# Gate products on an added weight, a matmul tile issued earlier, and the order of four engines around a recurrent attention block

## The reference, cut to what matters

```python
x = x + _L1_ffn_ref(_layernorm(x), ...)            # stage D: 256 -> 704 -> 256, gelu gate
x = x + _L2_xattn_ref(_layernorm(x), ctx, ctx, Wi, bi, Wf, bf, ln_scale)   # stage E
x = x + _L2_ffn_ref(_layernorm(x), weight, bias)   # stage F: ternary weights, 8-bit activations
x = x + _L3_xattn_ref(_layernorm(x), ctx, ...)     # stage G
```

```python
x = jnp.concatenate([q, k, v], axis=-1)            # k = v = ctx
ig = (x @ Wi + bi); fg = (x @ Wf + bf)             # 16 heads each
log_f = log_sigmoid(fg); log_f_cum = cumsum(log_f)
D = exp(log_D - max(log_D));  C = (q k^T) / 4 * D  # 64 heads (4 batches x 16)
h = (C / normaliser) @ v;  normalise per head
```

## Time and profile before

| | us |
|---|---|
| median of 3 runs (lowest, highest) | 1100.76 (1100.33, 1102.03) |
| the profiled execution, its own time | 1100.16 |
| its span in the profile | 1098.2 |
| PE, DVE, ACT, POOL busy | 1031.1, 873.1, 621.4, 567.2 |
| granted TensorE clock, mean | 0.984 |

### The profile page before, as it was taken

How to read it: one execution, slowest core, us unless ns; L and a number is a source line. 1 busy time by engine, 2 the same in 40 slices (tenths; PEclk the granted TensorE clock), 3 DMA queues, 4 the chain that set the end, 5 groups by cost and what they waited for, 6 DMA issues and landing times.

```text
span 1098.2 us, 19095 instructions
## 1 busy us (share of the span) xinstructions
PE 1031.1 (94%) x6570; PEld 877.5 (80%) x6570; DVE 873.1 (80%) x2154; ACT 621.4 (57%) x1657; POOL 567.2 (52%) x412
## 2 busy tenths in 40 slices
PE   8999999999998999889878999999999999999988
PEld 6458888888886786566556888998889988999976
DVE  6367777777778856599998888888887898888885
ACT  1774444444332356678656667665776666766643
POOL 4246666677652232044345665646565565655640
PEclk9999999999999999889989999999999999999999
DMA  7011101111000012000000101010100101000201
GB/s 268 1 46 66 58 29 58 37 52 58 30 1 27 1 56 77 2 1 1 20 1 19 59 1 40 1 59 1 34 7 2 58 2 39 2 20 1 88 1 39
DMA packets 15008, 37.43 MB, mean 34 GB/s; under 512 B 1649, under 2 KB 6849, under 8 KB 14401
## 3 DMA queue, kind: packets, MB, share of 16 engines
q1 hardware_dynamic: 14912, 36.21, 9.9%
HBM read 35.16 MB, written 1.05 MB: 33 GB/s over the span
## 4 chain that ended last, share of the span: by engine, by line
PE 66%; DVE 22%; ACT 6%; issue 4%; POOL 2%; DMA 0%; DVEq 0%; SPq 0%; ACTq 0%; POOLq 0%
PE bank L743 15%; PE bank L765 8%; PE bank L2160 8%; PE bank L2183 8%; PE bank L2091 7%; PE bank L2066 3%; PE bank L2102 3%; ACT y L2308 3%; PE bank L1126 2%; DVE g_ql L2025 2%; PE bank L2080 1%; DVE y L286 1%; DVE bst L249 1%; PE bank L531 1%; DVE arena L1625 1%
## 5 line engine op out<-in xcount | busy, mean ns | idle before, releaser
L2308 ACT ACTIVATE y<-bank,g_mx 128x256 f32<-128x256 f32 x256 | 117.2, 484 | 98.3 <-DVE g_mx L2471 98.3
L2586 POOL TENSOR_TENSOR y<-y,g_sm 128x1024 f32<-128x1024 f32 x64 | 120.2, 1899 | 23.9 <-DVE g_sm L2484 23.9
L2562 POOL TENSOR_TENSOR g_c<-arena 128x1024 fp32r<-128x1024 f32 x30 | 64.0, 2135 | 116.5 <-DVE arena L2405 116.5
L2183 PE MATMUL bank<-arena 128*128 128x256 f32 x512 | 116.1, 380 | 0.0
L795 ACT ACTIVATE arena<-arena 128x512 f32<-128x512 f32 x64 | 40.4, 632 | 120.6 <-DVE arena L880 120.5
L2183 PEld LDWEIGHTS bank<-arena 128*128 128x128 f32 x512 | 95.1, 190 | 11.9 <-issue 0.2
L743 PE MATMUL bank<-b_yh,b_wh 128*128 128x512 f32 x256 | 100.7, 393 | 0.0
L743 PE MATMUL bank<-b_yl,b_wh 128*128 128x512 f32 x256 | 100.0, 391 | 0.0
L743 PE MATMUL bank<-b_yh,b_wl 128*128 128x512 f32 x256 | 99.7, 390 | 0.0
L2066 PE MATMUL bank<-cst,y 128*128 128x128 f32 x512 | 74.0, 277 | 17.5 <-DVE x L2393 14.3
L831 POOL TENSOR_TENSOR b_hl<-arena,b_hh 128x512 fp32r<-128x512 f32 x64 | 81.3, 1291 | 9.6 <-ACT b_hh L804 9.6
(11 more groups left out here) (386 smaller groups left out, 3163.7 us busy)
## 6 DMA issues: line engine op xcount, KB each, us to landing
arena<-in_dram SPq DMA_DIRECT2D x37, 512.0 KB, 3.6
arena<-in_dram SPq DMA_DIRECT2D x18, 256.0 KB, 3.8
arena<-in_dram SPq DMA_DIRECT2D x3, 1024.0 KB, 4.9
arena<-in_dram SPq DMA_DIRECT2D x2, 704.0 KB, 6.0
x<-in_dram SPq DMA_DIRECT2D x4, 256.0 KB, 5.1
cx<-in_dram SPq DMA_DIRECT2D x4, 256.0 KB, 5.1
cxT<-in_dram SPq DMA_DIRECT2D x4, 256.0 KB, 5.4
cx<-in_dram SPq DMA_DIRECT2D x1, 1024.0 KB, 7.6
```

The costliest lines, as they stand in the source:

```text
L2183: m = pe.matmul(o[:, st * 256:st * 256 + 256], g_t[:, c, st * P:st * P + P], keys, start=True, stop=True)
L2308: m = act.activation(g_p[:, c, st, :], o[:, st * 256:st * 256 + 256], ACT.Exp, bias=g_mx[j % 2][:, 2 * c + st:2 * c + st + 1], accum_out=g ...
L2562: pool.tensor_tensor(cat, g_o[j % 2], g_om, ALU.subtract).then_inc(s_gc, 1)
L2586: pool.tensor_tensor(pf, pf, sums, ALU.mult).then_inc(s_gp, 1)
```

## The change

- **Gates.** The two weight blocks that meet the context are added once on POOL (`E_wsum_pool`, behind tile 3 of stage D). The first gate step on PE then makes the context products of all four batches (16 matmuls, four strips) and the products with `y` of batches 0 and 1 (8 matmuls). The second makes only the 8 with `y` of batches 2 and 3, into the same bank 0, which has held their context part since.
- **Order in stage D.** The products of the last hidden tile are issued right behind the one before, ahead of the gates; the down products of tiles 8 to 11 come behind the gates, and the value products behind all of them.
- **ACT.** Two one-column exponentials (`E_exp_act`) stand where nothing else waits, so that the table is loaded there; the logarithm of the gates comes between the two masked copies, behind the last hidden tile.
- **DVE.** Centring the values is cut in two around hidden tile 10; hidden tile 11 comes ahead of the gates, the last steps of stage F's weights behind them. The wait for `E_em_act` moves from `E_aT_dve` to the close of a batch.
- **Banks.** The decay tiles of steps 0 to 2 use banks 1 and 7, since bank 0 is held; from step 3 on banks 0 and 1.
- **Vector changes.** `F_quant_dve` clips only at 127, in one instruction with the subtraction (for each of four batches one instruction of 128x512 less). The four subtractions for stage G's first batch move from POOL to DVE (`G_first_inputs_dve`).

```diff
+        D_GU_AT = {n: (n,) for n in range(ND - 2)}
+        D_GU_AT[ND - 2] = (ND - 2, ND - 1)
...
+        ld_banks, ld_bank = (1, 7), 0
         for s_ in range(NQ + 1):
+            if s_ == 2:
+                plan(("E", "g", 1), 0)
+            if s_ == 3:
+                ld_banks = (0, 1)
...
-        def E_mask_act(act):
-            take(act, ("D", "gu", ND - 1, 1))
-            for odd in range(2):
-                act.activation(e_cm[odd], cxT[:, :, :], ACT.Identity, scale=cst[:, 312 + odd:313 + odd])\
-                    .then_inc(s_ecm, 1)
+        def E_mask_act(act, odd):
...
+        def E_exp_act(act, n):
+            if n:
+                act.wait_ge(s_eexp, n)
+            act.activation(e_r[:, 0, 0:1], mhalf[:, 0:1], ACT.Exp).then_inc(s_eexp, 1)
...
+        def E_wsum_pool(pool):
+            pool.wait_ge(s_wif, 16)
+            pool.tensor_tensor(e_wif[:, KD:2 * KD, :], e_wif[:, KD:2 * KD, :], e_wif[:, 2 * KD:3 * KD, :], ALU.add)\
+                .then_inc(s_wsum, 1)
...
         def E_gates_pe(pe, h):
+            o = claim(pe, ("E", "g", h))
             if h == 0:
-                pe.wait_ge(s_wif, 16)
-            o = claim(pe, ("E", "g", h))
-            for k in (2, 3, 4, 5, 0, 1):
...
+                pe.wait_ge(s_wsum, 1)
+                for k in range(KD):
+                    for gi_ in range(2):
+                        for b in range(B):
+                            pe.matmul(o[32 * b:32 * b + 32, gi_ * 256:gi_ * 256 + 256],
+                                      e_wif[:, KD + k, 32 * gi_:32 * gi_ + 32], cxT[:, k, b * 256:b * 256 + 256],
+                                      start=(k == 0 and gi_ == 0), stop=False, skip_group_check=True)
...
+            for k in range(KD):
                 for gi_ in range(2):
                     for b in (2 * h, 2 * h + 1):
...
+                                      yTh[:, h, k, b % 2 * 256:b % 2 * 256 + 256],
+                                      start=False, stop=(k == KD - 1), skip_group_check=True)
...
-            V.do(dve.tensor_scalar(f_v, f_v, ROUND23, -128.0, ALU.subtract, ALU.max))
-            V.sync()
...
-            dve.tensor_scalar(f_q, f_v, 127.0, None, ALU.min).then_inc(s_fq, 1)
+            dve.tensor_scalar(f_q, f_v, ROUND23 + 127.0, ROUND23, ALU.min, ALU.subtract).then_inc(s_fq, 1)
...
+        def G_first_inputs_dve(dve, p):
+            dve.wait_ge(s_gq, p + 1)
+            for v in (2 * p, 2 * p + 1):
...
+                dve.tensor_tensor(g_xs[v][:, 0, :, :], f, mb, ALU.subtract).then_inc(s_gx, 1)
...
@@ M_act @@
-                if n == ND:
-                    E_log_act(act, 0)
...
-            E_mask_act(act)
+            E_exp_act(act, 0)
+            E_mask_act(act, 0)
+            E_log_act(act, 0)
+            E_mask_act(act, 1)
             cross_v_act(act, 0, range(2))
+            E_exp_act(act, 1)
             E_em_act(act, 0)
@@ M_dve @@
             D_hidden_dve(dve, 10)
+            E_centred_dve(dve, V)
+            D_hidden_dve(dve, 11)
+            E_gates_dve(dve, V, 0)
             F_weights_last_dve(dve, V)
-            E_gates_dve(dve, V, 0)
-            D_hidden_dve(dve, 11)
             E_chain_dve(dve, V, 0)
@@ M_pool @@
+                if n == 3:
+                    E_wsum_pool(pool)
```

More of the change, by code:

```diff
@@ L987, in build @@
         for n in range(ND + 2):
-            if n < ND:
+            for m in D_GU_AT.get(n, ()):
                 for gu in range(2):
-                    plan(("D", "gu", n, gu), 4 + (2 * n + gu) % 4)
+                    plan(("D", "gu", m, gu), 4 + (2 * m + gu) % 4)
             if n >= 2 and (n - 2) % NI == 0:
@@ L1310, in E_prep_act @@
                     .then_inc(s_eprep, 1)
-        def E_mask_act(act):
-            take(act, ("D", "gu", ND - 1, 1))
-            for odd in range(2):
-                act.activation(e_cm[odd], cxT[:, :, :], ACT.Identity, scale=cst[:, 312 + odd:313 + odd])\
-                    .then_inc(s_ecm, 1)
+        def E_mask_act(act, odd):
+            if odd == 0:
+                take(act, ("D", "gu", ND - 1, 1))
+            act.activation(e_cm[odd], cxT[:, :, :], ACT.Identity, scale=cst[:, 312 + odd:313 + odd])\
+                .then_inc(s_ecm, 1)
+        def E_exp_act(act, n):
+            if n:
+                act.wait_ge(s_eexp, n)
+            act.activation(e_r[:, 0, 0:1], mhalf[:, 0:1], ACT.Exp).then_inc(s_eexp, 1)
         def E_y_act(act, batches):
@@ L1416, in E_aT_dve @@
                 .then_inc(s_em, 1)
-            have(dve, ("E", "tr", h))
         def E_parts_pool(pool, h):
@@ L1615, in E_centre_dve, with E_centred_dve @@
             V.do(dve.tensor_scalar(e_vm[:, :], e_vm[:, :], -1.0 / DH, None, ALU.mult))
+        def E_centred_dve(dve, V):
+            v3 = e_v.rearrange("p t h c -> p (t h) c")[:, :, 0:DH]
             V.sync()
@@ L1655, in E_dve @@
             take(dve, ("E", "hT", 2 * B - 1))
+            G_first_inputs_dve(dve, 0)
+            take(dve, ("E", "hv", B - 1, 1))
+            G_first_inputs_dve(dve, 1)
             E_close_dve(dve, V, 3)
@@ L1663, in E_close_dve @@
         def E_close_dve(dve, V, b):
+            have(dve, ("E", "tr", b // 2))
             have(dve, ("E", "hv", b, 0))
@@ L1710, in E_pool @@
             ln_pool(pool, C, K_F, EPS, batches=(2,))
-            take(pool, ("E", "hT", 2 * B - 1))
-            G_round_pool(pool, 0, (0,))
-            take(pool, ("E", "hv", B - 1, 1))
-            G_round_pool(pool, 0, (1,))
             ln_pool(pool, C, K_F, EPS, batches=(3,))
@@ L2872, in M_pe @@
             for n in range(ND + 2):
-                if n < ND:
-                    D_gu_pe(pe, n)
+                for m in D_GU_AT.get(n, ()):
+                    D_gu_pe(pe, m)
+                if n == 10:
+                    E_gates_pe(pe, 0)
                 if n in (2, 3):
```

41 lines of the change are left out of this document (18 added, 23 removed).

## The result

| | before | after |
|---|---|---|
| median of 4 runs, us | 1100.55 (1100.33 to 1102.03) | 1090.22 (1088.59 to 1091.11) |
| ratio | | 0.9902, 95% interval 0.9884 to 0.9919 |
| profiled execution, us (span) | 1100.16 (1098.2) | 1091.11 (1089.1) |
| mean granted clock | 0.984 | 0.987 |

What follows compares the result with a forecast made beforehand. A chain of waits passing between PE, ACT and DVE was taken to bound the loop, DVE stage G's entry; -3.7 - 2.9 - 1.8 - 0.9 = -9.3 us gave 1090.9, with 0.6 for the median 1091.5; 8 in 10 between 1088 and 1097.

Steps and rivals of the forecast that it cites:

- part 1: From stage D's gates to the loop's start: shorter context products and fewer waits, 3.7 us faster at the second step's scores.
- the wait of 0.74: PE's idle 0.74 us ahead of the transposes before the loop, claimed to go, with 1.0 us of cover.
- Part 2: Step 2 of the loop: 32 of 48 gate records go from PE, 2.9 us faster, bounds 1.4 to 3.5.
- bank 0's wait: Step 3's first decay tile waits for DVE to read the gates, until 451.5 instead of 454.39.
- Part 3: Stage F's quantisation, in the loop and at stage G's entry: four DVE instructions of 0.44 go, 1.8 us faster.
- Part 4: Stage G's entry: four subtractions add 2.6 us on DVE, which gets 3.5 back without POOL beside it; net 0.9 faster.
- Hidden work: POOL's weight sum, moved DVE steps and table preloads fall into idle time; without cover each preload would cost 1.28 + 0.2.
- half given back: Rival: the loop ends with DVE, whose own bound eats part of the earlier start; 5.5 us faster, 1095; chance 0.14.
- part 4 turned: Rival: at stage G's entry the four subtractions end later on DVE than on POOL; 5.8 us faster, 1095; chance 0.08.
- the slower clock: Rival: less PE work in the loop gives more idle time at the lower clock; 1103 or more; chance 0.03.
- the late logarithm: Rival: ACT reaches the gates' logarithm no earlier, behind a masked copy and tile 11; 1094.5; chance 0.08.
- the banks: Rival: waits for banks 0 and 7 in the loop cost 1.5 us more each; 6.3 us faster, 1094.4; chance 0.08.

## Why the prediction was right, step by step

The time (1091.5 forecast, 1090.22 measured) and the mechanism were right. That the sum comes so close is in part luck: part 1 was 1.0 us too large, and 1.28 us of the clock and 0.37 at the closing of batch 0, which no term held, made up for it.

- **Part 1 was too large: 3.7 forecast, 2.7 measured at step 1's scores.** The context products came out as chosen (1.94 against 1.9) and the wait of 0.74 went. But PE entered the loop 2.12 us earlier, not 2.5. The sum had left out small things: the gates take 1.73 us less from start to end, not 1.8; the transposes, which follow PE's work without a wait now, take 0.39 instead of 0.25 to the next product; and 0.14 us are lost in stage D to POOL's sum. The first exponential starts 0.68 us behind the first decay tile, as it did before (436.05 against 435.37), since ACT first copies the last value product; the forecast had put it 0.2 behind. And DVE's first product waits 0.79 us for scores which stand behind bank 7's wait. Both hang on the last value product: with it out of the way, step 1's scores come another 1.23 us earlier. Of the 2.74 us, the joined products brought 1.55, the moved wait 0.62, the order with the preloads 0.57. ACT's logarithm was no limit: DVE had ended the transposes' input (L1415) at 427.19, 3.1 us before PE came to them at 430.25, where the forecast had put 1.0.
- **Part 2 was right: 2.9 forecast, 3.0 between step 2's and step 3's scores** (8.30 to 5.27 us). The new limit is the one named, bank 0's wait behind DVE's two reads. Half of the removed records put back cost 1.72.
- **The clock was on the wrong side.** The forecast treated it only as a risk. In step 1 the kernel before ran at the lower clock behind its wait of 1.41 us, and lost 1.27 us that way, which filling the wait gives back. (In another execution with the same code up to there it lost 0.29 less, so the size depends on where the stretch falls.) The changed kernel waits 0.23 there and keeps the clock, so the gain jumps from 2.74 to 4.02 between two places with the same work. Less work did not bring more time at the lower clock, as the rival had it: with the waits shortened the mean rose from 0.91 to 0.95.
- **Part 3: 1.8 forecast, 1.83 measured,** in the line at all four places.
- **Part 4: 0.9 forecast, 0.91 to 1.07 measured.** The slow DVE instructions came and went with POOL's, as the rows of before had shown. The rule of the Trainium skill (SBUF — State Buffer, Who interferes with whom) that was weighed in the forecast, by which a GpSimd instruction that reads SBUF and such a Vector instruction shut each other out, is borne out: 1.26 us against 0.43, 3.46 against 1.67.
- **Hidden work.** The preloads are worth nothing. The forecast had POOL's sum hidden, and it was not quite: in all eleven profiles with it PE waits 0.34 or 0.35 us for DVE's L286, in the three without it 0.20.

Summed at stage G's second batch: 2.74 + 1.28 + 3.03 + 1.83 + 1.07 = 9.95 of the measured 10.32; the remaining 0.37 appears at the closing of batch 0 (7.41, behind 7.05 at the scores of step 3). That is the wait of 0.40 shown there, which the diff moves from behind the copy of the transposes to the closing. The forecast had not costed it; no experiment took it back by itself. Of the rivals, half given back, part 4 turned, the slower clock and the late logarithm are refuted by the same rows; the banks cost 0.40 and 0.35 us, not 1.5 each.

## What to carry to other kernels

Sum a chain over several engines place by place, counted from a place ahead of the change: where the places repeat within 0.03 us this separates terms of 0.5 us that whole times, uncertain by 1 to 2 us, do not. Find out with a second profile of the same kernel how far they do (here up to step 4; behind it 0.7 us). Before costing a shorter wait of PE, look at how fast the products behind it run: if they are at the lower clock, the wait costs more than its length, and a few idle products in it tell how much. When a sum of parts comes out right, check each part by itself: here one was a third too large and another was missing. Before moving work to the engine that a product waits for, read everything that stands ahead of that product on its own engine.

## What the hardware showed that was not expected

- Products without use inside a wait of PE paid for themselves in both places tried: 1.51 us of them ahead of step 1's scores brought 1.27 us at the next step, 2.43 us in step 4 brought 1.0, and neither delayed the work behind it by more than 0.02 us. In the times the first is clear of noise (1.1 us), the second is not (0.7).
- Matmuls of 32 output rows on four strips of the array take half as long a record as on two: 32 in 1.94 us, 16 in 1.92.
- A subtraction of 128x512 takes POOL 1.25 us and DVE 0.62, and while POOL is at it a mask instruction of DVE takes 1.26 us instead of 0.43 and four weight splits 3.46 instead of 1.67. DVE lost 3.4 us (2.49 + 0.91) to the 5 us of POOL's four subtractions. A sum of 128x128 on POOL (0.51 us) cost a scaling on DVE 0.14.
